# An attention slot in which the next head's q projection follows the longest scores

## The chip, the cores and the metric

The kernel runs on one core of a Trainium2 chip. The metric is the device time of one execution in microseconds (us), as the median of several runs.

## The reference

The input x has 8 batch items of 512 tokens and 256 channels. Three residual layers follow each other:

```
x = x + 0.5 * ffn(layernorm(x))
x = x + attention(layernorm(x))
x = x + 0.5 * ffn(layernorm(x))
```

The feed-forward layer is a gated mixture of 16 experts with its own causal attention inside. The attention in the middle, which this case is about, has 16 heads of 128 columns in 4 groups; the heads of a group share k and v:

```
q = x @ w_q;  k, v = split(x @ w_kv)
scores = q @ k.T * 128 ** -0.5, causal
out = softmax(scores) @ v, all heads @ w_dense
```

## The kernel before

All matrix products run in pairs of halves: a float32 value is kept as a high half (ScalarE's copy rounded to TensorE's format) and a low half (VectorE's remainder), and each product is three matmuls (`product`, line 1360: high by high, low by high, high by low). So every tile that TensorE makes passes first through ScalarE ("hi") and then VectorE ("lo") before TensorE can use it.

`attention` works in slots, one per head, 16 per item, 128 in all and 4 more to drain. The instruction order of each engine is written out by hand in that engine's own `slot(b, h)`; between engines only counting semaphores order the work, and each engine's queue is in order. In slot (b, h):

- TensorE: `attend` of the head four slots back (context = probabilities by v; "long" with 12 matmuls in even slots, "short" with 6 in odd ones, since two heads share the buffers), then the four score blocks of head h, `scores(now, 3)` to `scores(now, 0)`, for 512, 384, 256 and 128 key columns (the causal part of each 128 query rows), the projections that fall into places "B", "C" and "E", and `dense` for the head four back (12 matmuls), which waits for both halves of its context (`c_lo`).
- VectorE: the low halves of the previous head's probabilities (`split_probs`, line 1537), `score_max(now, 3)` (line 1520: adds the causal row and finds the maximum), the context's low half (`split_context`, line 1544), `score_max` of 2, 1 and 0, the low half of each projection (`split`, q at line 1503, k, v and z at 1505), and the sums' reciprocals (`prob_rsum`, lines 1528 and 1530). Scores 1 and 0 share a bank, so both maxima wait for scores 0. In slots 8 to 12 parts of the next item's layer norm follow.
- ScalarE: high halves of the previous head's probabilities (line 1614, wait for the factor of `prob_rsum`), of the context (line 1620), the four exponentials (line 1605, each waits for its maximum) and the high half of each projection (line 1599).
- GpSimd and the DMA queue transpose and cast the probabilities for the product two to four slots later.

Which projection falls where is the table `projections(h)`: the next head's q in place "B" of every slot from 0 to 14; v in place "C" of slots 0, 1 and 2 and in place "E" of slots 2, 4, 5, 6 and 8; k in "C" of slots 3, 7 and 11; in slots 14 and 15 the next item's z, q and k in "C" and "E". Place "B" stands before scores 1 on TensorE, behind all four maxima on VectorE and behind exponential 2 on ScalarE:

```
                place("B")
                if now:
                    exponential(now, 1)
                place("C")
                if now:
                    exponential(now, 0)
                place("D")
```

The lines 1516 (a causal sum ahead of maximum 0), 1397 and 1399 (scores 0, two matmuls) belong to the shortest block.

Of the kernel before, what the change touches and what calls it, by code (L numbers as in the profile page):

```python
# [25 lines left out]
B, SEQ, C = 8, 512, 256  # L26
# [1182 lines left out]
def attention(nc, m, aw):  # L1209
    with ExitStack() as ctx:  # L1210
# [145 lines left out]
        def _(pe):  # L1356
# [88 lines left out]
            def slot(b, h):  # L1445
                now, last = unit(b, h, 0), unit(b, h, LAST_LAG)

                def place(p):
                    what = projections(h).get(p)
                    if what and has_projection(b, h, what):  # L1450
                        project(b + 1 if h >= 14 and what in NEXT_ITEM else b, use_index(b, h, p), what)

                if last:
                    attend(last)
                if now:
                    scores(now, 3)
                    scores(now, 2)
                place("B")
                if now:
                    scores(now, 1)  # L1460
                    scores(now, 0)
                place("C")
                done = last if b < B else unit(b, h, LAST_LAG + 1) if h else None
                if done:
                    dense(done, 0)
                place("D")
                if done:
                    dense(done, 1)
                place("E")
                place("F")  # L1470
                if b == B and h == LAST_LAG - 1:
                    dense(last, 0)
                    dense(last, 1)
# [5 lines left out]
        @block.vector  # L1479
        def _(dve):  # L1480
            def layer_norm(b, t):
                T = (b - 1) * QT + t
                dve.bn_stats(stats[:, t], tile_of(m.x, b * QT + t)).then_inc(stats_done, 1)
                dve.wait_ge(stats_done, T + 1)

                reach(dve, var_done, T - QT + 1)
                settle(dve)
                dve.bn_aggr(mv[:, t], stats[:, t]).then_inc(mv_done, 1)

            def layer_norm_apply(b, t):  # L1490
                T = (b - 1) * QT + t
                dve.wait_ge(rstd_done, T + 1)
                if b > 1:

                    dve.wait_ge(pj_ready, use_of(b - 1, ("z", t // 2)) + 1)
                dve.tensor_scalar(z[:, t], tile_of(m.x, b * QT + t), mv[:, t, 0:1], rstd[:, t:t + 1],
                                  ALU.subtract, ALU.mult).then_inc(z_done, 1)

            def split(n, what):
                raw, hi, lo = use_halves(n, what)  # L1500
                dve.wait_ge(pj_hi, n + 1)
                if what[0] == "q":
                    dve.scalar_tensor_tensor(lo, raw, SCALE, as_f32(hi), ALU.mult, ALU.subtract).then_inc(pj_lo, 1)  # L1503
                else:
                    dve.tensor_tensor(lo, raw, as_f32(hi), ALU.subtract).then_inc(pj_lo, 1)  # L1505

            def score_max(u, i):
                _, h, n = u
                dve.wait_ge(s_ready, QT * n + turn_of(i if i > 1 else 0) + 1)

                reach(dve, p_lo, done_of(n - 1, i))
                at, width = PROB_AT[i], (i + 1) * P
                raw = scores_at(i, 0, width)
                row = m.causal[:, SEQ - width:]
                if i == 0:
                    dve.tensor_tensor(expo[:, 0:P], scores_at(0, P, 2 * P), row, ALU.add).then_inc(s_summed, 1)
                    dve.wait_ge(s_summed, n + 1)
                    row = expo[:, 0:P]
                settle(dve)
                dve.tensor_tensor_reduce(expo[:, at:at + width], raw, row,  # L1520
                                         -1.0, BIGGEST, ALU.add, ALU.min,
                                         s_bias[:, h % 2, i:i + 1]).then_inc(s_max, 1)

            def prob_rsum(u, i):
                _, h, n = u
                dve.wait_ge(e_done, done_of(n, i))
                half = slice(i, i + 2)
                dve.reciprocal(p_rsum[:, h % 2, half], p_sum[:, h % 2, half]).then_inc(r_done, 1)
                dve.wait_ge(r_done, 4 * n + 3 - i)
                dve.tensor_scalar(p_factor[:, h % 2, half], p_rsum[:, h % 2, half], PROB_SCALE, None,  # L1530
                                  ALU.mult).then_inc(r_done, 1)

            def split_probs(u, i):
                _, h, n = u
                dve.wait_ge(p_hi, done_of(n, i))
                at, width = PROB_AT[i], (i + 1) * P
                dve.scalar_tensor_tensor(prob_half(1, i), expo[:, at:at + width].rearrange("p (j k) -> p j k", k=P),  # L1537
                                         p_factor[:, h % 2, i:i + 1], prob_half(0, i),
                                         ALU.mult, ALU.subtract).then_inc(p_lo, 1)

            def split_context(u):
                _, h, n = u
                dve.wait_ge(c_hi, n + 1)
                dve.scalar_tensor_tensor(ctx_half(n, 1), ctx_bank(n)[:], 1.0 / PROB_SCALE, as_f32(ctx_half(n, 0)),  # L1544
                                         ALU.mult, ALU.subtract).then_inc(c_lo, 1)

            def add_to_x(b, half):
                dve.wait_ge(d_ready, 2 * b + 2 - half)
                x = m.x[:, b * QT + 2 * half:b * QT + 2 * half + 2, :].rearrange("p t c -> p (t c)")
                dve.tensor_tensor(x, x, dn[half][:], ALU.add).then_inc(x_added, 1)  # L1550

            def slot(b, h):
                now, prev, last = unit(b, h, 0), unit(b, h, 1), unit(b, h, LAST_LAG)

                def place(p):
                    what = projections(h).get(p)
                    if what and has_projection(b, h, what):
                        split(use_index(b, h, p), what)

                if prev:  # L1560
                    prob_rsum(prev, 0)
                    for i in reversed(range(QT)):
                        split_probs(prev, i)
                if now:
                    score_max(now, 3)
                if last:
                    split_context(last)
                if now:
                    score_max(now, 2)
                    score_max(now, 1)  # L1570
                    score_max(now, 0)
                place("B")
                if now:
                    prob_rsum(now, 2)
                place("C")
                place("D")
                place("E")
                if not (isinstance(b, int) and b >= B - 1):

                    if 8 <= h < 12:  # L1580
                        layer_norm(b + 1, h - 8)
                    if 9 <= h < 13:
                        layer_norm_apply(b + 1, h - 9)
                place("F")
                if h == LAST_LAG - 2 and last and b < B or h == LAST_LAG - 1 and b == B:
                    add_to_x(b - 1, 1)
                if h == LAST_LAG - 1 and last:
                    add_to_x(b - 1, 0)

            for n, what in enumerate(PROLOGUE):  # L1590
                split(n, what)
            attention_slots(slot)(dve)

        @block.scalar
        def _(act):
# [5 lines left out]
            def exponential(u, i):  # L1601
                _, h, n = u
                act.wait_ge(s_max, done_of(n, i))
                at, width = PROB_AT[i], (i + 1) * P
                act.activation(expo[:, at:at + width], expo[:, at:at + width], ACT.Exp, bias=s_bias[:, h % 2, i:i + 1],  # L1605
                               scale=-1.0, accum_out=p_sum[:, h % 2, i:i + 1]).then_inc(e_done, 1)
# [15 lines left out]
            def slot(b, h):  # L1622
                now, prev, last = unit(b, h, 0), unit(b, h, 1), unit(b, h, LAST_LAG)

                def place(p):
                    what = projections(h).get(p)
                    if what and has_projection(b, h, what):
                        split(use_index(b, h, p), what)
# [7 lines left out]
                    aw.split_hi(act, EARLY + LATE - 1, wd, stage)  # L1636
                if now:
                    exponential(now, 3)
                    exponential(now, 2)
                place("B")  # L1640
                if now:
                    exponential(now, 1)
                place("C")
                if now:
# [104 lines left out]
```

## Time and profile before

| | |
|---|---|
| median of 3 runs | 2592.98 us (2592.41 to 2593.59) |
| the profiled execution | 2595.07 us, its span 2593.2 us |
| TensorE matmuls busy | 2499.9 us, 96% |
| VectorE busy | 2153.8 us, 83% |
| ScalarE busy | 944.7 us, 36% |
| mean granted TensorE clock | 0.988 of full speed |
| attention stage | about 820 to 1780 us of the span |

In the profile PE is TensorE's matmul, PEld its weight load, DVE VectorE, ACT ScalarE, POOL GpSimd. L1520 is line 1520 of the kernel. A bracket at the end of a timeline row is the engine's idle time just before it and the instruction that ended it. Matmuls overlap, so a group's time ends after the next group's start.

### The profile page before, as it was taken

Reading aid. Unit: us, or ns where it says so; the run is one execution under the profiler, and the core shown is the slowest. Engines: PE = TensorE matmul, PEld = TensorE weight load, DVE = VectorE, ACT = ScalarE, POOL = GpSimd, SP = SyncE. Lnnn points to the kernel's source line nnn. Section 1 sums busy time; section 2 is a strip of 40 time slices with the busy share of each in tenths; the row PEclk is TensorE's granted clock in tenths of the full one; section 3 lists DMA queues with packets and bytes.
Section 4 is the critical chain, followed back from the end, with each engine's and each line's share of the span. In section 5 each row is a group of like instructions: output and inputs, shape, how many; then the busy total and the mean of one; then the engine's idle time right before and its main releaser. Section 6 shows DMA issues by size and latency. Waiting matters only on the chain. (4 is left out here: it accounts for less than half of the span.)

```text
span 2593.2 us, 45059 instructions
## 1 busy us (share of the span) xinstructions
PE 2499.9 (96%) x13966; PEld 2285.9 (88%) x13966; DVE 2153.8 (83%) x6164; ACT 944.7 (36%) x2546; POOL 954.5 (37%) x2010
## 2 busy tenths in 40 slices
PE   6999999999997999999999999997999999999998
PEld 6999999999995888888888888886899999999997
DVE  6888888888886888888888888886888888888887
ACT  3111101101103777777777777774111101101100
POOL 4333333333334434343434444344333333333331
PEclk9999999999998999999999999998999999999999
DMA  6000000000012544454554545455100000000000
GB/s 190 11 8 9 6 8 9 6 8 9 10 36 62 92 88 90 89 93 92 87 90 90 92 92 89 86 98 129 39 9 18 12 9 18 13 9 18 15 6 22
DMA packets 419056, 127.08 MB, mean 49 GB/s; under 512 B 378880, under 2 KB 417792, under 8 KB 418816
## 3 DMA queue, kind: packets, MB, share of 16 engines
q1 hardware_dynamic: 418816, 124.20, 24.1%
q8 instruction: 112, 1.84, 0.3%
q14 instruction: 128, 1.05, 0.1%
HBM read 26.24 MB, written 4.19 MB: 12 GB/s over the span
## 5 line engine op out<-in xcount | busy, mean ns | idle before, releaser
L583 PE MATMUL ffn_ring<-ffn_mix_weights,ffn_yT 128*128 128x384 f32 x5760 | 1133.2, 341 | 6.7 <-DVE ffn_mix_weights L828 4.0
L583 PEld LDWEIGHTS ffn_ring<-ffn_mix_weights,ffn_yT 128*128 128x128 f32 x5760 | 1008.6, 189 | 53.1 <-DVE ffn_mix_sums L757 17.9
L759 DVE SCALAR_TENSOR_TENSOR ffn_mix_sums<-ffn_ring,ffn_w,ffn_mix_sums 128x384 f32<-128x384 f32 x896 | 551.7, 616 | 229.1 <-PE ffn_ring L583 207.0
L637 PE MATMUL ffn_ring<-ffn_out_weights,ffn_avT 128*128 128x512 f32 x1536 | 443.3, 399 | 7.5 <-POOL ffn_avT L1085 5.7
L1605 ACT ACTIVATE attn_exponentials<-attn_exponentials,attn_score_neg_max 128x512 f32<-128x512 f32 (+3 forms) x512 | 285.8, 559 | 164.3 <-DVE attn_score_neg_max L1520 163.7
L1673 POOL CAST attn_probsT_long<-attn_turned_long 128x1024 fp32r<-128x1024 f16 (+1 forms) x256 | 233.1, 939 | 253.6 <-DVE attn_probs L1537 253.1
L637 PEld LDWEIGHTS ffn_ring<-ffn_out_weights,ffn_avT 128*128 128x128 f32 x1536 | 283.0, 189 | 37.9 <-POOL ffn_avT L1085 7.4
L1537 DVE SCALAR_TENSOR_TENSOR attn_probs<-attn_exponentials,attn_prob_factor,attn_probs 128x512 f16<-128x512 f32 (+3 forms) x512 | 248.2, 546 | 17.3 <-ACT attn_probs L1614 17.0
L1614 ACT ACTIVATE attn_probs<-attn_exponentials,attn_prob_factor 128x512 f16<-128x512 f32 (+3 forms) x512 | 250.2, 552 | 25.0 <-DVE attn_prob_factor L1530 15.8
L924 ACT ACTIVATE ffn_yT<-ffn_transposes 128x256 fp32r<-128x256 f32 x64 | 24.6, 384 | 639.6 <-PE ffn_transposes L553 639.6
L774 DVE SCALAR_TENSOR_TENSOR x<-ffn_ring,ffn_w_out,x 128x256 f32<-128x256 f32 x512 | 246.5, 481 | 13.0 <-PE ffn_ring L637 7.3
L1360 PE MATMUL attn_scores<-attn_kT,attn_qT 128*128 128x512 f32 (+2 forms) x1152 | 242.8, 338 | 4.7 <-DVE attn_qT L1503 3.2
L1520 DVE CUSTOM_DVE_ANT_0 attn_exponentials<-attn_scores,causal_row 128x512 f32<-128x512 f32 (+2 forms) x384 | 205.7, 550 | 34.1 <-PE attn_scores L1399 25.4
L1360 PEld LDWEIGHTS attn_scores<-attn_kT,attn_qT 128*128 128x128 f32 x1152 | 197.6, 189 | 33.8 <-DVE attn_qT L1503 3.6
L1360 PE MATMUL attn_dense<-attn_wd,attn_ctxT 128*128 128x256 f32 x1512 | 201.8, 283 | 23.1 <-DVE attn_ctxT L1544 22.3
L1360 PEld LDWEIGHTS attn_dense<-attn_wd,attn_ctxT 128*128 128x128 f32 x1512 | 185.0, 189 | 33.6 <-DVE attn_ctxT L1544 31.6
L778 DVE SCALAR_TENSOR_TENSOR ffn_out_odd<-ffn_ring,ffn_w_out,ffn_out_odd 128x256 f32<-128x256 f32 x448 | 212.7, 475 | 0.0
L1673 POOL CAST attn_probsT_short<-attn_turned_short 128x512 fp32r<-128x512 f16 (+1 forms) x256 | 123.6, 512 | 230.2 <-DVE attn_probs L1537 230.2
L1360 PE MATMUL attn_projections<-attn_zT,early_wq 128*128 128x512 f32 x768 | 202.8, 400 | 1.5 <-DVE attn_zT L1505 1.5
L928 ACT ACTIVATE ffn_qT<-ffn_transposes 128x128 fp32r<-128x128 f32 x64 | 17.9, 279 | 453.3 <-PE ffn_transposes L593 453.3
L1360 PE MATMUL attn_ctx<-attn_probsT_long,attn_v 128*128 128x512 f32 (+1 forms) x768 | 168.8, 369 | 1.1 <-POOL attn_probsT_long L1673 1.1
L1360 PEld LDWEIGHTS attn_projections<-attn_zT,early_wq 128*128 128x128 f32 x768 | 143.8, 190 | 25.3 <-DVE attn_zT L1505 1.9
(152 smaller groups left out, 3145.0 us busy)
## 6 DMA issues: line engine op xcount, KB each, us to landing
ffn_mix_stage<-in_L_ffn_q_proj_dram SPq DMA_DIRECT2D x32, 128.0 KB, 2.6
ffn_mix_stage<-in_L_ffn_k_proj_dram SPq DMA_DIRECT2D x32, 128.0 KB, 2.6
ffn_mix_stage<-in_L_ffn_v_proj_dram SPq DMA_DIRECT2D x32, 128.0 KB, 2.9
ffn_out_stage<-in_L_ffn_o_proj_dram SPq DMA_DIRECT2D x16, 256.0 KB, 2.9
out_dram<-x SPq DMA_DIRECT2D x8, 512.0 KB, 3.1
x<-in_L_attn_x_dram SPq DMA_DIRECT2D x7, 512.0 KB, 8.8
early_stage<-in_L_attn_w_q_dram SPq DMA_DIRECT2D x4, 512.0 KB, 5.1
attn_dense_stage<-in_L_attn_w_dense_dram SPq DMA_DIRECT2D x4, 512.0 KB, 4.5
```

The lines of the kernel that those rows point to most:

```text
L583: last = pe.matmul(bank[:, 0:QKV], yT[:, t % 2, h, k * P:(k + 1) * P], mix_half(e, wh)[:, k], start=(n == 0), stop=(n == 3 * CK - 1))
L637: last = pe.matmul(bank[:], avT[:, t % 2, h], wo[:, g, wh], start=(i == 0), stop=(i == 2))
L759: dve.scalar_tensor_tensor(into, bank[:, 0:QKV], w[:, t, e:e + 1], into, ALU.mult, ALU.add).then_inc(mix_done, 1)
L774: dve.scalar_tensor_tensor(x, bank[:, 0:C], wt[:, 2 * g:2 * g + 1], x, ALU.mult, ALU.add)
L778: dve.scalar_tensor_tensor(odd[:, t % 2], bank[:, C:2 * C], wt[:, 2 * g + 1:2 * g + 2], odd[:, t % 2], ALU.mult, ALU.add).then_inc(out_don ...
L924: act.activation(yT[:, t % 2, 0], tr[:, 0:C], ACT.Copy).then_inc(yT_hi, 1)
L1360: mm = pe.matmul(out_ap, stationary(a), moving(c), start=first and n == 0, stop=last and n == 2, skip_group_check=True)
L1520: dve.tensor_tensor_reduce(expo[:, at:at + width], raw, row, -1.0, BIGGEST, ALU.add, ALU.min, s_bias[:, h % 2, i:i + 1]).then_inc(s_max, 1)
L1537: dve.scalar_tensor_tensor(prob_half(1, i), expo[:, at:at + width].rearrange("p (j k) -> p j k", k=P), p_factor[:, h % 2, i:i + 1], prob_h ...
L1605: act.activation(expo[:, at:at + width], expo[:, at:at + width], ACT.Exp, bias=s_bias[:, h % 2, i:i + 1], scale=-1.0, accum_out=p_sum[:, h ...
L1614: act.activation(prob_half(0, i), expo[:, at:at + width].rearrange("p (j k) -> p j k", k=P), ACT.Copy, scale=p_factor[:, h % 2, i:i + 1]). ...
L1673: pool.tensor_copy(cast(n, i), landed(n, i).rearrange("p (j h q) -> p j h q", h=HL, q=P)).then_inc(long_cast if pair_of(i) else short_cast, 1)
```

## The change

Place "B" moves up by one score block on TensorE and by one exponential on ScalarE, so that it stands directly behind block 3 on both. On VectorE it moves up by two maxima and stands between maximum 2 and maximum 1. Nothing else is different.

```
@@ tensor, slot @@
                 if now:
                     scores(now, 3)
-                    scores(now, 2)
                 place("B")
                 if now:
+                    scores(now, 2)
                     scores(now, 1)
                     scores(now, 0)
@@ vector, slot @@
                 if now:
                     score_max(now, 2)
+                place("B")
+                if now:
                     score_max(now, 1)
                     score_max(now, 0)
-                place("B")
                 if now:
                     prob_rsum(now, 2)
@@ scalar, slot @@
                 if now:
                     exponential(now, 3)
-                    exponential(now, 2)
                 place("B")
                 if now:
+                    exponential(now, 2)
                     exponential(now, 1)
```

## Rows read from the trace of the kernel before

**Rows 1.** Busy time: one item, all eight; after the us PE, PEld, DVE, ACT, POOL
```profile
1409.00:1526.00 117.00, 114.38 (x690) 101.49 (x689) 101.39 (x333) 90.54 (x239) 47.12 (x72) 1.00 0.50 91
...
sum 930.00, PE 903.13 PEld 800.67 DVE 797.92 ACT 717.19 POOL 374.01; mean PE 112.89 PEld 100.08 DVE 99.74 ACT 89.65 POOL 46.75
```
**Rows 2.** Waits, 870 to 1780 us: total us, times, longest us
```profile
PEld attn_dense L1360 <- DVE attn_ctxT L1544: 31.4, 43, 2.5
DVE attn_exponentials L1520 <- PE attn_scores L1399: 23.1, 44, 0.7
PE attn_dense L1360 <- DVE attn_ctxT L1544: 22.3, 32, 2.4
DVE attn_qT L1503 <- ACT attn_qT L1599: 21.1, 75, 0.5
```
**Rows 3.** Timeline of slot 13, sixth item: start, us, instruction, idle before
```profile
1514.04 0.68 DVE L1520 CUSTOM_DVE_ANT_0 attn_exponentials<-attn_scores,causal_row 128x512 f32<-128x512 f32 x1
...
1514.77 0.72 ACT L1605 ACTIVATE attn_exponentials<-attn_exponentials,attn_score_neg_max 128x512 f32<-128x512 f32 x1 [0.94 <-DVE attn_score_neg_max L1520]
...
1515.26 0.55 DVE L1520 CUSTOM_DVE_ANT_0 attn_exponentials<-attn_scores,causal_row 128x384 f32<-128x384 f32 x1
1515.39 1.65 PE L1360 MATMUL attn_dense<-attn_wd,attn_ctxT 128*128 128x256 f32 x12 [0.80 <-DVE attn_ctxT L1544]
...
1515.73 0.42 DVE L1520 CUSTOM_DVE_ANT_0 attn_exponentials<-attn_scores,causal_row 128x256 f32<-128x256 f32 x1
1515.85 0.62 ACT L1605 ACTIVATE attn_exponentials<-attn_exponentials,attn_score_neg_max 128x384 f32<-128x384 f32 x1 [0.26 <-DVE attn_score_neg_max L1520]
...
1516.46 0.58 ACT L1599 ACTIVATE attn_qT<-attn_projections 128x512 fp32r<-128x512 f32 x1
1516.50 0.29 DVE L1520 CUSTOM_DVE_ANT_0 attn_exponentials<-attn_scores,attn_exponentials 128x128 f32<-128x128 f32 x1
...
1516.94 0.50 ACT L1605 ACTIVATE attn_exponentials<-attn_exponentials,attn_score_neg_max 128x256 f32<-128x256 f32 x1
1517.08 0.69 DVE L1503 SCALAR_TENSOR_TENSOR attn_qT<-attn_projections,attn_qT 128x512 fp32r<-128x512 f32 x1 [0.27 <-ACT attn_qT L1599]
...
1517.43 0.39 ACT L1605 ACTIVATE attn_exponentials<-attn_exponentials,attn_score_neg_max 128x128 f32<-128x128 f32 x1
...
1518.08 1.23 ACT L1614 ACTIVATE attn_probs<-attn_exponentials,attn_prob_factor 128x512 f16<-128x512 f32 x2 [0.16 <-DVE attn_prob_factor L1530]
...
1518.83 0.75 DVE L1537 SCALAR_TENSOR_TENSOR attn_probs<-attn_exponentials,attn_prob_factor,attn_probs 128x512 f16<-128x512 f32 x1 [0.52 <-ACT attn_probs L1614]
```
**Rows 4.** Timeline of slot 8, same item
```profile
1476.71 1.38 PE L1360 MATMUL attn_scores<-attn_kT,attn_qT 128*128 128x512 f32 x6
...
1477.93 1.56 PE L1360 MATMUL attn_projections<-attn_zT,early_wq 128*128 128x512 f32 x6
...
1478.97 0.55 DVE L1520 CUSTOM_DVE_ANT_0 attn_exponentials<-attn_scores,causal_row 128x384 f32<-128x384 f32 x1
...
1480.19 0.42 DVE L1520 CUSTOM_DVE_ANT_0 attn_exponentials<-attn_scores,causal_row 128x256 f32<-128x256 f32 x1 [0.67 <-PE attn_scores L1399]
```
**Rows 5.** Timeline, end of slot 4 and the dense product of slot 5
```profile
1452.61 0.39 ACT L1605 ACTIVATE attn_exponentials<-attn_exponentials,attn_score_neg_max 128x128 f32<-128x128 f32 x1
...
1453.15 0.39 ACT L1599 ACTIVATE attn_v<-attn_projections 128x256 fp32r<-128x256 f32 x1
...
1453.57 0.42 DVE L1505 TENSOR_TENSOR attn_v<-attn_projections,attn_v 128x256 fp32r<-128x256 f32 x1 [0.35 <-ACT attn_v L1599]
...
1457.39 0.77 PEld L1360 LDWEIGHTS attn_dense<-attn_wd,attn_ctxT 128*128 128x128 f32 x6 [0.23 <-DVE attn_ctxT L1544]
```
**Rows 6.** Timeline of slot 11, same item: the k halves
```profile
1503.09 0.58 ACT L1599 ACTIVATE attn_kT<-attn_projections 128x512 fp32r<-128x512 f32 x1
...
1503.70 0.69 DVE L1505 TENSOR_TENSOR attn_kT<-attn_projections,attn_kT 128x512 fp32r<-128x512 f32 x1
```
**Rows 7.** Busy time where the slots begin; the number behind POOL is the clock
```profile
838.00:846.00 8.00, 5.91 (x27) 4.94 (x26) 7.10 (x22) 5.53 (x15) 4.76 (x2) 0.82 0.44 82
```

More of the change, by code:

```diff
@@ L1456, in slot @@
                     scores(now, 3)
-                    scores(now, 2)
                 place("B")
                 if now:
+                    scores(now, 2)
                     scores(now, 1)
@@ L1569, in slot @@
                     score_max(now, 2)
+                place("B")
+                if now:
                     score_max(now, 1)
                     score_max(now, 0)
-                place("B")
                 if now:
@@ L1638, in slot @@
                     exponential(now, 3)
-                    exponential(now, 2)
                 place("B")
                 if now:
+                    exponential(now, 2)
                     exponential(now, 1)
```

## The prediction

> **What bounds the kernel.** I read the stretches of the attention stage first, then its list of waits, then the timelines of single slots. TensorE is busy 903 of the 930 us of the attention stage; one batch item of 16 slots takes about 117 us, and TensorE is busy 114 of them [rows 1]. So whatever only rearranges the other engines can gain no more than TensorE's idle time, and the change adds or removes no matmul. Who ends that idle time: the dense product waits for VectorE's low half of the context, 22.3 us by the matmul row, 31.4 us in 43 waits by the weight-load row, which sees the start of each wait sooner [rows 2]. 43 waits in some 124 slots: about two slots in three have none. The feed-forward stages hold none of the edited lines. The question is how much earlier or later VectorE delivers the context half in the slots where TensorE stands waiting for it.
>
> I read slot 13 (no second projection, no layer norm on VectorE) with its first maximum, 1514.04, as zero [rows 3]. VectorE: maximum 3 (of the longest block) at 0, then the context half, maximum 2 at 1.22, maximum 1 at 1.69, maximum 0 at 2.46, idle until ScalarE's q half is there, q low half at 3.04. Maximum 2 of 0.55 makes room for the next operation after 0.47, 0.08 before its end; so too maximum 0 (0.29) makes room at 2.68 and the q low half (0.69) at 3.64. ScalarE: exponential 3 at 0.73, exponential 2 at 1.81, q half at 2.42, exponential 1 at 2.90, exponential 0 at 3.39, over at 3.78. It idles 0.16 more for the factor, starts the probabilities at 4.04, and VectorE, after 0.52 of idle time, starts its splits at 4.79. The next slot's maximum 3 stands behind four such splits and the context half behind that; the dense product had waited 0.80 for it here. This loop through VectorE and ScalarE, not TensorE, sets the pace of slots 9 to 13. In other slots VectorE waits for scores instead: 0.67 in slot 8 [rows 4], 23.1 us in all [rows 2].
>
> **The change, part by part.** (a) TensorE: the q projection stands ahead of scores 2. In slot 8, scores 3 and 2 take 1.22 from start to start [rows 4]: 0.69 and 0.53 by their columns; the projection, twice scores 3, takes 1.40. So scores 2 is first issued at 1476.71 + 0.69 + 1.40 = 1478.80 and its maximum starts about 0.87 later (maximum 3 came 1.04 after its three matmuls of 0.23; these are of 0.18), at 1479.67. Before, it ran at 1478.97 and VectorE then waited until 1480.19. The wait moves ahead of maximum 2, and behind it come 0.47 (maximum 2) + 0.60 (q low half) + 0.77 (maximum 1 and the causal sum) + 0.22 = 2.06, which ends at 1481.73; before, 1480.19 + 0.77 + 0.22 + 0.60 = 1481.78. Cost nothing; the cover is the wait for scores.
>
> (b) VectorE where it sets the pace. The q half starts when exponential 3 is through, at 0.73 + 0.72 = 1.45, takes 0.58, and the low half starts at 2.05. VectorE is free at 1.69, so it waits 0.36 there; before it was free at 2.68 and started at 3.04, 0.36 as well. Then 0.60 + 0.77 + 0.22: the section closes at 3.64, where it closed before [rows 3]. The wait for the q half (21.1 us in all [rows 2]) changes its place and is no gain.
>
> (c) ScalarE's last exponential loses its cover. Maximum 0 moves from 2.46 to 3.42. Exponential 0 follows a maximum by its length and 0.05 for the flag (0.73 after 0.68), so it starts at 3.42 + 0.34 = 3.76, was 3.39, and ends at 4.15. The probabilities start at 4.15, was 4.04, and the splits at 4.91, was 4.79: +0.12 where nothing else stands between.
>
> (d) Where a second projection follows, ScalarE's queue is in the way. Maximum 1 starts at 2.65, exponential 1 at 3.12, and it ends at 3.61 instead of 3.39. The k half behind it (slots 3, 7, 11) goes 0.22 later, and the k low half, which follows it closely [rows 6], with it: +0.22. In slot 4 the v half comes behind exponential 0. That ran at 1452.61, and the v half at 1453.15 [rows 5], released by TensorE. Now the slot begins 0.22 late (slot 3's k half), exponential 0 runs at 1452.61 + 0.37 + 0.22 = 1453.20 to 1453.59, and the v half starts 0.44 late. VectorE had stood waiting 0.35 for it, so all splits come 0.44 late; slot 5's dense product had waited 0.23 already [rows 5], so TensorE pays it whole.
>
> (e) Layer norm on VectorE (in slots 8 to 12) stands between this section and the splits and covers (c) in slots 9 and 10; in slot 12 only a short piece of it is left, and the probabilities wait there as in slot 13. If that cover failed, each would cost 0.12.
>
> **The sum.** A normal item pays slot 4's 0.44, slot 11's 0.22 and slot 12's 0.12: 0.78 us of new waiting at the dense products of slots 5, 12 and 13. The slips of the other slots fall on slots whose dense product does not wait, or behind VectorE's wait for scores. Seven items: 5.5. The last item has no layer norm: 0.44 and twice 0.12 make 0.7. Together 6.2. The slots that fill the pipeline I take as zero: TensorE gets its q low half 0.99 sooner, but VectorE's maxima there follow its own splits.
>
> The clock in that stretch is granted at 0.82 of full speed in the mean [rows 7], so part of it runs at 1.2 GHz instead of 2.4. The Trainium skill ("TensorE: Matmul & The Clock Gate", Part 1) says that the gate opens by recent activity. By that rule, products that stand closer together there might keep 2.4 GHz and shorten matmuls that nobody waits for; by the row the term is zero either way.
>
> The profiled execution took 2595.07 (span 2593.2 and 1.9 around it), 0.08% over the median of 2592.98. The sum gives 2601.3 for a profiled one, and for the median 2592.98 + 6.2 = 2599.2.
>
> [...]
>
> **Bounds of what no row shows.** Nowhere does the q half follow exponential 3. At best it starts at 1.45 (behind exponential 2, of 0.62, it came after 0.61). At worst it first waits as long again as ScalarE needs to hand over a sum; the longest such stretch in rows 3 is the 0.16 of idle time before the probabilities. That is 0.16 in each of six paced slots, 1 us an item, +8. I take 1.45, from the nearer row. On the other side the 0.44 and 0.12 could be nothing if slots 5 and 13 have slack that I misread: then 0.22 an item, +1.8.
>
> **Rivals.** *Absorbed:* the late exponentials fall into slack and at most the k slips stay: 0 to +3, 2593 to 2596. For it: two slots in three have slack. Against: rows 3 and 5 show both receivers already waiting. *Faster:* VectorE's wait for the q half vanishes. One point decides: the q half must be complete by 1.69 after the first maximum. Then the section closes 0.35 sooner, the splits 0.24 to 0.35 sooner in slots 9 to 12, and the dense waits shrink by up to 1.3 an item: 2592.98 - 9 = 2584. For it: the 75 waits of rows 2. Against: 0.73 + 0.72 + 0.58 = 2.03. *Costlier:* the 0.37 of exponential 0 reaches the next slot whole in slots 8 to 13, by the handing over or an order of ScalarE's queue that I misread: 6 x 0.37 + 0.44 = 2.7 an item, less what slack takes, +12 to +19: 2605 to 2612. Against: the layer norm and the factor wait of 0.16 lie between.
>
> **Chances.** Forecast (+4 to +11) 0.57; absorbed 0.2; faster 0.09; costlier 0.14. The likeliest time is 2599.2. The range, 2589 to 2608, takes in the absorbed case and the +8 of the worse bound on top of the sum, and leaves out most of the faster and the upper part of the costlier case. A measurement of this kernel tells about 0.2%, 5.2 us, from no change. Slower than 2598.2: the costlier case and most of the forecast, 0.6; within 0.2%: 0.3; faster: 0.1.
>
> **What would show it.** In the profile after: VectorE's idle time before the q low half still about 0.27, now behind maximum 2; the 23.1 us of waiting for the last scores gone, and as much for scores 2 in its place; no factor wait of ScalarE in slots 12 and 13; slot 4's v low half 0.4 later; the dense product's wait up from 22.3 to about 28 us; TensorE's busy time the same. The prediction is wrong if the dense wait falls, or if the q half starts well away from 1.45.

## The result, and the profile after

The changed kernel takes 2597.89 us (median of 19 runs, 2594.52 to 2604.02), the kernel before 2590.47 us (19 runs beside them, 2584.89 to 2594.14). The ratio is 1.0029 with a 95% interval of 1.0023 to 1.0036: slower by 7.4 us, where 6.2 was predicted (2599.2, in a range of 2589 to 2608). The forecast had been added to a median of three runs, 2592.98; the 19 runs put the kernel before 2.5 us lower.

The page's first part, for the changed kernel:

```profile
PE 2494.8 (96%) x13966; PEld 2282.9 (88%) x13966; DVE 2157.0 (83%) x6164; ACT 944.1 (36%) x2546; POOL 951.6 (37%) x2010
```

The counts of instructions are those of before. The attention item of [rows 1] again, now cut exactly from the first maximum of its slot 0 to that of the next item, for the kernel before:

```profile
1419.29:1536.37 117.08, 114.46 (x690) 101.57 (x689) 101.45 (x333) 90.61 (x238) 47.12 (x72) 1.00 0.50 91
```

and the changed kernel:

```profile
1421.62:1539.65 118.03, 114.29 (x689) 101.59 (x689) 101.88 (x333) 90.47 (x238) 47.02 (x72) 1.00 0.49 90
```

TensorE's work is the same and the item is 0.95 us longer. Eight such items would make 7.6 us. This item length is used below beside the medians, since it leaves out all that varies elsewhere in a run; in both kernels ScalarE waits for no late transpose in the sixth item, while it does in some others. The seven whole items, cut in the same way, are longer by 0.84, 0.67, 1.15, 0.80, 0.94, 0.95 and 0.18 us, and the last, up to the first maximum of its last slot, by 1.36: together 6.9 us from the first such maximum of the stage to the last.

The list of waits that answers to [rows 2], changed kernel, attention stage:

```profile
PEld attn_dense L1360 <- DVE attn_ctxT L1544: 41.1, 47, 3.4
PE attn_dense L1360 <- DVE attn_ctxT L1544: 32.0, 40, 3.2
DVE attn_qT L1503 <- ACT attn_qT L1600: 25.5, 84, 0.5
DVE attn_exponentials L1520 <- PE attn_scores L1360: 18.1, 38, 0.7
ACT attn_probs L1615 <- DVE attn_prob_factor L1530: 8.5, 23, 1.0
```

TensorE waits 41.1 us for the context's low half instead of 31.4. The wait for the last scores (line 1399, 23.1 us) has left the list. In its place stand 18.1 us for line 1360, of which 17.4 are waits of maximum 2 for scores 2, where as much as 23.1 was forecast. Before, the row of line 1360 had 7.2 us, all of them waits of maximum 3 for scores 3, and of these 0.7 are left. The wait for the q half is still there. Slot 13 of the same item, to be laid beside [rows 3]; its first maximum is at 1517.27:

```profile
1517.27 0.69 DVE L1520 CUSTOM_DVE_ANT_0 attn_exponentials<-attn_scores,causal_row 128x512 f32<-128x512 f32 x1
...
1518.00 0.72 ACT L1606 ACTIVATE attn_exponentials<-attn_exponentials,attn_score_neg_max 128x512 f32<-128x512 f32 x1 [0.94 <-DVE attn_score_neg_max L1520]
...
1518.48 0.55 DVE L1520 CUSTOM_DVE_ANT_0 attn_exponentials<-attn_scores,causal_row 128x384 f32<-128x384 f32 x1
1518.62 1.68 PE L1360 MATMUL attn_dense<-attn_wd,attn_ctxT 128*128 128x256 f32 x12 [0.91 <-DVE attn_ctxT L1544]
1518.72 0.58 ACT L1600 ACTIVATE attn_qT<-attn_projections 128x512 fp32r<-128x512 f32 x1
...
1519.33 0.69 DVE L1503 SCALAR_TENSOR_TENSOR attn_qT<-attn_projections,attn_qT 128x512 fp32r<-128x512 f32 x1 [0.29 <-ACT attn_qT L1600]
...
1520.71 0.29 DVE L1520 CUSTOM_DVE_ANT_0 attn_exponentials<-attn_scores,attn_exponentials 128x128 f32<-128x128 f32 x1
...
1521.04 0.40 ACT L1606 ACTIVATE attn_exponentials<-attn_exponentials,attn_score_neg_max 128x128 f32<-128x128 f32 x1
...
1521.44 1.21 ACT L1615 ACTIVATE attn_probs<-attn_exponentials,attn_prob_factor 128x512 f16<-128x512 f32 x2
...
1522.19 0.75 DVE L1537 SCALAR_TENSOR_TENSOR attn_probs<-attn_exponentials,attn_prob_factor,attn_probs 128x512 f16<-128x512 f32 x1 [0.24 <-ACT attn_probs L1615]
```

Counted from the first maximum: q half at 1.45 (predicted 1.45), q low half at 2.06 (2.05), maximum 0 at 3.44 (3.42), exponential 0 at 3.77 (3.76), probabilities at 4.17 (4.15), splits at 4.92 (4.91; before 4.79). The 0.29 in front of the q low half is the old 0.27 in a new place. The factor wait in front of the probabilities is gone: what holds them now is exponential 0.

### The profile page after: what moved, and what is told of

Same layout as the page of the kernel before. It is cut to its first block and busy times, and to the rows that moved or that the text cites. A ratio compares the mean times of both kernels' runs of the same rounds, so it can differ in the third digit from the quotient of the medians.

```text
span 2597.1 us, 45059 instructions
## 1 busy us (share of the span) xinstructions
PE 2494.8 (96%) x13966; PEld 2282.9 (88%) x13966; DVE 2157.0 (83%) x6164; ACT 944.1 (36%) x2546; POOL 951.6 (37%) x2010
## 5 line engine op out<-in xcount | busy, mean ns | idle before, releaser
L1360 PEld LDWEIGHTS attn_scores<-attn_kT,attn_qT 128*128 128x128 f32 x1152 | 193.0, 188 | 22.3 <-DVE attn_qT L1503 3.2
```

Of the source, the lines that this page charges most:

```text
L1360: mm = pe.matmul(out_ap, stationary(a), moving(c), start=first and n == 0, stop=last and n == 2, skip_group_check=True)
```

## The experiments

Item length is from first maximum to first maximum of the sixth item, as above (start and end in us of each run's span); time against the kernel before is the ratio of medians with its 95% interval.

| run | TensorE | VectorE | ScalarE | median us | before, run beside it | ratio | item |
|---|---|---|---|---|---|---|---|
| before | old | old | old | 2590.47 | | 1 | 1419.29 to 1536.37: 117.08 |
| changed | new | new | new | 2597.89 | 2590.47 | 1.0029 (1.0023 to 1.0036) | 1421.62 to 1539.65: 118.03 |
| pe_only | new | old | old | 2596.40 | 2589.55 | 1.0025 (1.0015 to 1.0035) | 1419.01 to 1536.84: 117.83 |
| dve_act | old | new | new | 2598.62 | 2589.55 | 1.0037 (1.0025 to 1.0050) | 1421.47 to 1539.45: 117.98 |
| act_only | old | old | new | 2581.76 | 2589.55 | 0.9971 (0.9959 to 0.9982) | 1414.11 to 1530.24: 116.13 |
| pe_act | new | old | new | 2582.36 | 2589.55 | 0.9970 (0.9960 to 0.9980) | 1409.42 to 1525.48: 116.06 |
| pe_dve | new | new | old | 2704.59 | 2589.67 | 1.0442 (1.0423 to 1.0462) | 1487.62 to 1620.39: 132.77 |
| pe_only_but_2_14 | new but in two slots | old | old | 2592.73 | 2589.67 | 1.0011 (1.0003 to 1.0020) | 1417.82 to 1535.03: 117.21 |
| after_k_first | new | new | new, k half sooner | 2592.37 | 2589.67 | 1.0010 (1.0001 to 1.0019) | 1418.13 to 1535.52: 117.39 |
| after_v_first | new | new | new, v half sooner | 2596.89 | 2592.53 | 1.0018 (1.0009 to 1.0027) | 1420.49 to 1538.42: 117.93 |
| dve_between_1_and_0 | new | between 1 and 0 | new | 2579.08 | 2589.67 | 0.9956 (0.9943 to 0.9970) | 1410.98 to 1527.08: 116.10 |
| dve_between_pe_before | old | between 1 and 0 | new | 2580.14 | 2592.53 | 0.9953 (0.9941 to 0.9966) | 1407.82 to 1523.92: 116.10 |

### Each engine's part by itself

The first four kernels are made of the diff's three hunks, each taken or left: `pe_only` has the first, `dve_act` the second and third, `act_only` the third, `pe_act` the first and third. `pe_dve`, further down, has the first and second. VectorE's hunk without either of the others was not run.

**pe_only.**

> Only TensorE's part of the change: the q projection ahead of scores 2, while VectorE and ScalarE keep the order of before. Theory (the lateness comes from ScalarE's last exponential and the halves queued behind it): no change, within 1 us of the kernel before; in slots where VectorE waits for scores the wait of 0.67 us moves ahead of maximum 2 and the section closes at the same time; dense wait near 22 us. Rival (the later scores 2 themselves delay the maxima and through them the loop): 5 to 8 us slower, with a dense wait near 30 us.

Measured 1.0025, 6.9 us: the time is the rival's, but neither theory named what happened. The item is 0.75 longer, yet TensorE's wait for the context half is 22.7 us by the matmul row (22.3 before) and 32.0 by the weight-load row (31.4 before), so the rival's dense wait did not come. Slot 14 of the sixth item in this kernel shows the place:

```profile
1522.44 0.56 DVE L1520 CUSTOM_DVE_ANT_0 attn_exponentials<-attn_scores,causal_row 128x384 f32<-128x384 f32 x1 [0.33 <-PE attn_scores L1360]
...
1523.04 0.62 ACT L1605 ACTIVATE attn_exponentials<-attn_exponentials,attn_score_neg_max 128x384 f32<-128x384 f32 x1 [0.68 <-DVE attn_score_neg_max L1520]
...
1523.66 0.58 ACT L1599 ACTIVATE attn_qT<-attn_projections 128x512 fp32r<-128x512 f32 x1
...
1524.27 0.69 DVE L1503 SCALAR_TENSOR_TENSOR attn_qT<-attn_projections,attn_qT 128x512 fp32r<-128x512 f32 x1 [0.22 <-ACT attn_qT L1599]
...
1525.01 0.42 PEld L1374 LDWEIGHTS attn_projections<-ident,attn_z 128*128 128x128 f32 x4 [0.59 <-DVE attn_qT L1503]
```

Scores 2 come late, so maximum 2 is late, so exponential 2 is late, and the q half, queued behind exponential 2 in the old ScalarE order, is late with it. TensorE waits 0.59 (0.28 before) for the q low half before it can transpose z. The second v product of slot 2 waits for the q low half in the same way, 0.30, where none is listed for it before. From 870 to 1780 us these waits of TensorE's projections for the q low half are 6.6 us (4.1 and 2.5, seven times each) against 2.5 before. I had followed the late scores along VectorE only, and not along ScalarE's queue.

**dve_act.**

> VectorE's and ScalarE's parts of the change, with TensorE's order of before (scores 2 ahead of the q projection). Theory: all of the loss, 6 to 8 us slower than before, since the slots that set the pace never wait for scores; slots 12 and 13 take 6.77 us from first maximum to first maximum, as in the changed kernel, against 6.65 before. Rival (scores 2 behind the projection is what costs): within 2 us of the kernel before.

As the theory had it: 1.0037, slots 12 and 13 of 6.77 and 6.76, an item of 117.98 against 118.03 for the whole change. With ScalarE's part in place TensorE's order makes no difference that shows (0.05 an item).

**act_only.**

> ScalarE's q half ahead of exponential 2, VectorE's q low half left behind all four maxima, TensorE as before. Theory: in slots that VectorE and ScalarE pace, the q half is ready at 2.03 us after the first maximum, VectorE is free for it at 2.68 and no longer waits 0.36; exponential 0 is not pushed back (2.46 + 0.34, behind exponential 1 it starts at about 3.04); the section closes 0.36 sooner and slots 12 and 13 take about 6.3 us instead of 6.65. Gain about 1.4 us an item, 8 to 12 us in all, 2579 to 2583 beside 2590.5. Rival (any move of the q half ahead of exponential 2 delays the exponentials and so the next slot): slower than before by 3 to 8 us.

Measured 7.8 us faster, just under the 8 to 12 expected, and the rival is out. VectorE's wait for the q half falls from 21.1 to 3.4 us and the dense wait from 31.4 to 23.7. Slots 12 and 13 take 6.33 and 6.31 as expected, but the item is only 0.95 shorter instead of 1.4; slot 14, at 8.23 instead of 7.90, gives 0.33 back. Slot 13, first maximum at 1507.91:

```profile
1509.36 0.58 ACT L1599 ACTIVATE attn_qT<-attn_projections 128x512 fp32r<-128x512 f32 x1
...
1510.37 0.29 DVE L1520 CUSTOM_DVE_ANT_0 attn_exponentials<-attn_scores,attn_exponentials 128x128 f32<-128x128 f32 x1
...
1510.59 0.69 DVE L1503 SCALAR_TENSOR_TENSOR attn_qT<-attn_projections,attn_qT 128x512 fp32r<-128x512 f32 x1
...
1511.58 1.23 ACT L1614 ACTIVATE attn_probs<-attn_exponentials,attn_prob_factor 128x512 f16<-128x512 f32 x2 [0.17 <-DVE attn_prob_factor L1530]
...
1512.34 0.75 DVE L1537 SCALAR_TENSOR_TENSOR attn_probs<-attn_exponentials,attn_prob_factor,attn_probs 128x512 f16<-128x512 f32 x1 [0.52 <-ACT attn_probs L1614]
```

The q half is ready at 2.03, maximum 0 is out of the way at 2.68, the low half starts there with no idle time, and the splits at 4.43 instead of 4.79.

**pe_act.**

> TensorE's and ScalarE's parts of the change, VectorE's q low half left behind all four maxima. Theory: as with ScalarE's part alone, 8 to 12 us faster than before; the q projection comes sooner on TensorE, so in slots led by TensorE the q half no longer holds up exponential 2, worth 0 to 2 us more. Rival (scores 2 behind the projection costs by itself): several us slower than ScalarE's part alone.

The same time as `act_only` (0.9970 and 0.9971; items of 116.06 and 116.13). TensorE's part costs 0.75 an item with ScalarE's old order and nothing with its new one, because the q half no longer stands behind exponential 2.

### Where TensorE's part alone costs

```
                     scores(now, 3)
+                    if h in (2, 14):
+                        scores(now, 2)
                 place("B")
                 if now:
+                    if h not in (2, 14):
+                        scores(now, 2)
                     scores(now, 1)
```

> TensorE's part alone cost 6.8 us, which I had not expected. Theory now: with scores 2 late, exponential 2 is late on ScalarE, and the q half, which stands behind it, is 0.7 us late too; that reaches TensorE only where it needs the q low half at once, for the second v product of slot 2 and the second z transposes of slot 14, 0.3 us each. Here TensorE keeps the order of before in slots 2 and 14 and has the new one elsewhere: within 1.5 us of the kernel before. Rival (the late scores cost a little in every slot): 4 to 6 us slower than before.

The item is 117.21: of the 0.75, 0.62 goes away with two slots of sixteen. The time is 3.1 us above before with an interval of 0.8 to 5.2, which is not within the 1.5 expected at its middle and does not exclude it. TensorE's projections wait 2.7 us for the q low half here, against 6.6 in `pe_only` and 2.5 before: 3.9 us of waiting go, and the time falls by 3.8. The places are shown; where the remaining 3.1 us come from is not.

### ScalarE's queue in the changed kernel

**after_k_first**, against the changed kernel (and "C" left out of its old place in these slots):

```
                     exponential(now, 2)
+                if h in (3, 7, 11):
+                    place("C")
+                if now:
                     exponential(now, 1)
```

> The changed kernel, with ScalarE's k half of slots 3, 7 and 11 ahead of exponential 1 instead of behind it. Theory (a second projection's half waits behind the delayed exponential 1): the 0.22 to 0.24 of slots 3 and 11 go away, slot 11 takes about 7.7 us again instead of 7.95, slot 5's dense product waits 0.2 less; 3 us of the 7.4 come back, 2594 to 2596 beside 2590.5. Rival (the loss comes from exponential 0 alone): the same as the changed kernel within 1 us.

1.0010, 2.7 us above before instead of 7.4: 4.7 us came back, more than the 3 forecast. The item is 0.64 shorter than the changed kernel's, and slot 5's dense product waits 0.39 instead of 0.67. Slot 11 of the changed kernel, first maximum at 1502.56:

```profile
1505.68 0.51 ACT L1606 ACTIVATE attn_exponentials<-attn_exponentials,attn_score_neg_max 128x256 f32<-128x256 f32 x1 [0.50 <-DVE attn_score_neg_max L1520]
1506.19 0.58 ACT L1600 ACTIVATE attn_kT<-attn_projections 128x512 fp32r<-128x512 f32 x1
1506.67 0.39 ACT L1606 ACTIVATE attn_exponentials<-attn_exponentials,attn_score_neg_max 128x128 f32<-128x128 f32 x1
1506.80 0.69 DVE L1505 TENSOR_TENSOR attn_kT<-attn_projections,attn_kT 128x512 fp32r<-128x512 f32 x1 [0.23 <-ACT attn_kT L1600]
```

and of this kernel, first maximum at 1498.75:

```profile
1501.27 0.58 ACT L1600 ACTIVATE attn_kT<-attn_projections 128x512 fp32r<-128x512 f32 x1
1501.87 0.51 ACT L1606 ACTIVATE attn_exponentials<-attn_exponentials,attn_score_neg_max 128x256 f32<-128x256 f32 x1
...
1502.67 0.68 DVE L1505 TENSOR_TENSOR attn_kT<-attn_projections,attn_kT 128x512 fp32r<-128x512 f32 x1
```

Behind exponential 1 the k low half starts at 4.24; ahead of it at 3.92, sooner even than the 4.01 of the kernel before ([rows 6], first maximum at 1499.69). So the change had cost 0.23 there, close to the forecast 0.22, and this edit gives that back and 0.09 more, in slot 3 as in slot 11. It costs nothing: exponential 1 starts 3.12 after the first maximum in both kernels, since the k half fits into time in which ScalarE waits 0.50 for maximum 1.

**after_v_first**, against the changed kernel:

```
+                if 4 <= h <= 8:
+                    place("E")
                 if now:
                     exponential(now, 0)
                 place("D")
-                place("E")
+                if not 4 <= h <= 8:
+                    place("E")
```

> The changed kernel, with ScalarE's v half of slots 4, 5, 6 and 8 ahead of exponential 0 instead of behind it. The prediction laid slot 4's 0.44 on the v half waiting behind exponential 0. Theory now: both gates close at the same time. With the v half first, at 1453.15, exponential 0 runs from 1453.44 to 1453.83, the first probabilities are there at 1454.55 and the splits start at 1454.58 instead of 1454.62 (times of the kernel before, slot 4): no gain, within 1.5 us of the changed kernel, 2596 to 2599 beside 2590, and slot 5's dense product still waits about 0.65. Rival (the place of the v half alone makes the 0.44): 3 us faster than the changed kernel, slot 5 waits about 0.25.

By the rows of the sixth item the theory holds: the item is 117.93 (118.03 changed), and slot 5's dense product waits 0.60 there, against 0.67. Slot 4 of the changed kernel and the dense product that pays for it, to be laid beside [rows 5]:

```profile
1455.48 0.40 ACT L1606 ACTIVATE attn_exponentials<-attn_exponentials,attn_score_neg_max 128x128 f32<-128x128 f32 x1
...
1455.88 0.36 ACT L1600 ACTIVATE attn_v<-attn_projections 128x256 fp32r<-128x256 f32 x1
...
1456.28 0.42 DVE L1505 TENSOR_TENSOR attn_v<-attn_projections,attn_v 128x256 fp32r<-128x256 f32 x1 [0.55 <-ACT attn_v L1600]
...
1460.09 0.30 PEld L1360 LDWEIGHTS attn_dense<-attn_wd,attn_ctxT 128*128 128x128 f32 x2 [0.67 <-DVE attn_ctxT L1544]
```

and slot 4 with the v half first:

```profile
1454.34 0.38 ACT L1600 ACTIVATE attn_v<-attn_projections 128x256 fp32r<-128x256 f32 x1
1454.62 0.39 ACT L1606 ACTIVATE attn_exponentials<-attn_exponentials,attn_score_neg_max 128x128 f32<-128x128 f32 x1
...
1455.01 1.22 ACT L1615 ACTIVATE attn_probs<-attn_exponentials,attn_prob_factor 128x512 f16<-128x512 f32 x2
1455.75 0.75 DVE L1537 SCALAR_TENSOR_TENSOR attn_probs<-attn_exponentials,attn_prob_factor,attn_probs 128x512 f16<-128x512 f32 x1 [0.24 <-ACT attn_probs L1615]
...
1458.95 0.19 PEld L1360 LDWEIGHTS attn_dense<-attn_wd,attn_ctxT 128*128 128x128 f32 x1 [0.60 <-DVE attn_ctxT L1544]
```

VectorE waits 0.18 for the v half instead of 0.55, and 0.24 more for the probabilities, which stand behind exponential 0. The edit does not open one gate and leave the other: exponential 0 now starts 4.07 after the first maximum of the slot instead of 3.78. The splits start at 5.20 here and at 5.18 in the changed kernel. There, too, the two gates close together: its probabilities start at 1456.14, and with the 0.74 that lie between probabilities and splits here, that gives 1456.88, which is when VectorE, through with the v half and the reciprocals behind it, starts its splits. The time does not settle it. 4.4 us above before against 7.4 looks like the rival's 3 us, but the intervals, 1.0009 to 1.0027 and 1.0023 to 1.0036, overlap, and in the profiled executions 2.6 us of the difference lie in the fourth item alone (118.76 against 121.37), where the changed kernel has late transposes.

### VectorE's part, smaller and larger

**dve_between_1_and_0**, against the changed kernel:

```
                     score_max(now, 2)
+                    score_max(now, 1)
                 place("B")
                 if now:
-                    score_max(now, 1)
                     score_max(now, 0)
```

> The changed kernel, with VectorE's q low half between maximum 1 and maximum 0 instead of between 2 and 1. Theory: VectorE is free at 2.03 after the first maximum and the q half is there at 2.03, so no wait is left; maximum 0 starts at about 3.08, exponential 0 at 3.42, the splits at about 4.57 instead of 4.91; slots 12 and 13 take 6.4 us instead of 6.77; the kernel is 6 to 9 us faster than before, near the one with ScalarE's and TensorE's parts alone. Rival (every low half ahead of a maximum costs its length, 0.6, by way of exponential 0): slower than before.

The fastest in this study beside its twin below: 0.9956, 10.6 us under before, more than the 6 to 9 expected; slots 12 and 13 take 6.43 each. VectorE's wait for the q half falls from 21.1 us before to 3.3. Slot 13, first maximum at 1505.01:

```profile
1507.07 0.69 DVE L1503 SCALAR_TENSOR_TENSOR attn_qT<-attn_projections,attn_qT 128x512 fp32r<-128x512 f32 x1
...
1508.11 0.29 DVE L1520 CUSTOM_DVE_ANT_0 attn_exponentials<-attn_scores,attn_exponentials 128x128 f32<-128x128 f32 x1
...
1508.44 0.40 ACT L1606 ACTIVATE attn_exponentials<-attn_exponentials,attn_score_neg_max 128x128 f32<-128x128 f32 x1 [0.32 <-DVE attn_score_neg_max L1520]
...
1509.58 0.75 DVE L1537 SCALAR_TENSOR_TENSOR attn_probs<-attn_exponentials,attn_prob_factor,attn_probs 128x512 f16<-128x512 f32 x1 [0.24 <-ACT attn_probs L1615]
```

The low half starts at 2.06 with no idle time in front. One maximum further back, and the sign of the change turns: with the gap ahead of the low half the whole chain behind it is late (splits at 4.92); without the gap exponential 0 starts at 3.43, only 0.04 later than before, and the splits at 4.57, as computed (4.79 before).

**dve_between_pe_before** is the same with TensorE's old order.

> ScalarE's q half ahead of exponential 2, VectorE's q low half between maximum 1 and maximum 0, TensorE in the order of before. Theory: TensorE's part is worth next to nothing once ScalarE's part is there: 8 to 12 us faster than before, as with TensorE's part, and an item takes 116.1 us between first maxima. Rival (the q projection ahead of scores 2 helps where TensorE leads): only 4 to 7 us faster than before.

0.9953, 12.4 us under before, and an item of 116.10, the same to 0.01 us. The two intervals overlap nearly whole. TensorE's order is worth nothing here.

**pe_dve**, ScalarE's hunk left out:

> TensorE's and VectorE's parts of the change, with ScalarE's q half left behind exponential 2. Theory: VectorE then stands in front of the q low half until 3.04 after the first maximum, 1.35 after it is free, and the section closes near 4.6 instead of 3.64: about 1 us in every slot that VectorE and ScalarE pace, and most slots become such; 50 to 90 us slower than before, with 70 to 130 us of waiting for the q half. Rival (such waits fall into slack, as two slots in three have some): under 20 us slower.

115 us slower, more than the 50 to 90 expected. In slot 13 (first maximum at 1595.20) the low half is held as computed, to 3.03:

```profile
1598.23 0.69 DVE L1503 SCALAR_TENSOR_TENSOR attn_qT<-attn_projections,attn_qT 128x512 fp32r<-128x512 f32 x1 [1.26 <-ACT attn_qT L1600]
```

Slots 4 to 7 take 8.0 to 8.1 each (6.8 to 7.4 before), VectorE waits 148 us for the q half from 870 us on (70 to 130 expected), and the item is 15.7 us longer, 0.98 a slot: the price per slot was near the 1 us computed, and nearly every slot pays it, not only 50 to 90 of the 128. Against `pe_only`, which differs in VectorE's order alone, the loss is 108 us or 0.85 a slot, and ScalarE's order has to buy it back.

## Why the prediction was right, point by point

*What bounds the kernel.* Held. TensorE's work did not move (114.46 and 114.29 us an item), and the loss appears as waiting of the dense product.

*(a), TensorE's part at no cost.* Right inside the whole change (`dve_act` has the same item within 0.05), wrong as a statement of its own. By itself it costs 0.75 an item by way of exponential 2 and the q half. It is free only because ScalarE's hunk takes the q half out from behind exponential 2. In slot 8 the move of the wait came out as computed; these rows are of the changed kernel, whose first maximum there is at 1480.49:

```profile
1482.42 0.56 DVE L1520 CUSTOM_DVE_ANT_0 attn_exponentials<-attn_scores,causal_row 128x384 f32<-128x384 f32 x1 [0.62 <-PE attn_scores L1360]
...
1482.90 0.69 DVE L1503 SCALAR_TENSOR_TENSOR attn_qT<-attn_projections,attn_qT 128x512 fp32r<-128x512 f32 x1
```

Maximum 2 at 1.93, predicted 1479.67 - 1477.75 = 1.92.

*(b), the section closes where it did.* Held to 0.02 in slot 13. The lower bound (the q half right behind exponential 3) is what the chip does: 1.45, and the worse bound of 0.16 a slot is out.

*(c), exponential 0.* Held: 0.12 in slot 12, and 0.13 more before the splits of slot 13. `dve_between_1_and_0` and `act_only` turn the sign by taking away VectorE's gap ahead of the q low half, which shows that the gap, with maximum 0 behind it, is what makes exponential 0 late in the paced slots.

*(d), the second projections.* Slot 5's dense product pays 0.67 - 0.23 = 0.44, the predicted 0.44. The reason given was only half of it: the late v half is one of two gates that close together, and the other is the same late exponential 0 with the probabilities behind it. Putting the v half first, which moves that exponential back, gained 0.07. The k halves were sized right: the k low half of slot 11 is 0.23 later, and slots 3 and 11 are 0.23 and 0.24 longer, where 0.22 was forecast. `after_k_first` takes more than that off because it puts the k half sooner than it had been before the change.

*The sum.* 0.78 an item was forecast and 0.95 came. From first maximum to first maximum, slots 0 to 2 are 0.09 shorter together and slots 3 to 5 0.52 longer (0.44 forecast), slots 6 to 10 0.11 longer (nothing forecast), slots 11 and 12 0.24 and 0.12 (0.22 and 0.12 forecast), slot 13 0.12, and slots 14 and 15 0.07 shorter. So the mis-sized terms are small ones around those named: slots 8 and 9, which I set at zero, cost 0.07 (dense wait of slot 9 0.92, was 0.85), and slot 13's 0.12, which I let fall into slack, did not quite vanish. The dense product of slot 12 waits 0.28 longer, 0.22 forecast; before and after:

```profile
1508.75 0.41 PEld L1360 LDWEIGHTS attn_dense<-attn_wd,attn_ctxT 128*128 128x128 f32 x3 [0.60 <-DVE attn_ctxT L1544]
1511.86 0.30 PEld L1360 LDWEIGHTS attn_dense<-attn_wd,attn_ctxT 128*128 128x128 f32 x2 [0.88 <-DVE attn_ctxT L1544]
```

The rows of slots 14 and 15, before:

```profile
1524.54 0.20 PEld L1374 LDWEIGHTS attn_projections<-ident,attn_z 128*128 128x128 f32 x2 [0.28 <-DVE attn_qT L1503]
...
1529.93 0.19 PEld L1360 LDWEIGHTS attn_dense<-attn_wd,attn_ctxT 128*128 128x128 f32 x1 [0.93 <-DVE attn_ctxT L1544]
```

and after:

```profile
1533.22 0.19 PEld L1360 LDWEIGHTS attn_dense<-attn_wd,attn_ctxT 128*128 128x128 f32 x1 [1.24 <-DVE attn_ctxT L1544]
```

The sooner q low half did free TensorE's z transposes (0.28 of waiting, gone), and the dense product of slot 15 waits 0.31 longer: what was gained was given back a slot later. The dense waits rose more than forecast (32.0 us, forecast about 28) mostly for this reason: slot 15 alone has 0.32 more in the matmul row (0.81, was 0.49), 2.6 us in eight items.

Part of the close agreement is luck. The seven whole items sum to 5.53 us where 5.5 was forecast, but only because the seventh, at 0.18, makes up for what the undisturbed ones pay above 0.78; the last item pays 1.36 where 0.7 was forecast. And 2599.2 lies 1.3 us above the measured median, while the kernel before came out 2.5 us below the figure that it was added to.

*The clock.* In the stretch of [rows 7] the changed kernel was granted 1.00 where the kernel before had 0.82, and its low stretch lies later (0.62 from 848 to 852 us). The first item was 0.84 longer all the same, so nothing here shows a gain from the clock; no run isolates it.

*The rivals.* "Absorbed" is out by the interval. "Costlier" is out: the factor wait and the layer norm stood between, as said. "Faster" named the right mechanism, VectorE's idle time before the q low half, and rightly said that this change does not remove it; `act_only` and `dve_between_1_and_0` remove it and gain 7.8 and 10.6 us, near the 9 that this rival was given. The deciding point was that the q half be complete by 1.69; it is complete at 2.03, and one maximum later VectorE reaches the low half at 2.06 without a wait.

## What to carry to other kernels

These are lessons from one kernel. When one stage is made of an early half on one engine and a late half on another, move the early half forward and let the late half follow only so far that its engine need not wait for it; moved further, the late half takes its wait along and puts both in front of whatever used to come ahead of it. Follow a moved instruction down every in-order queue that it or its neighbours' inputs stand in, also those of engines whose order is not edited. Where two gates close at the same time, opening one shows little: change both, or read which one closes next.

## What the runs showed that was not expected

TensorE's reordering alone, which delays one score block by 1.4 us and nothing else on that engine, made the kernel 0.25% slower (1.0015 to 1.0035) through ScalarE's queue, two engines away. And in `pe_dve` VectorE stands still in front of a low half that starts when it did before (3.03 after the first maximum in slot 13, 3.04 before), with two maxima now behind it instead of ahead of it, and that costs 115 us over 128 slots, 0.9 us a slot: the slack that two dense products in three had absorbed little of it.
